# x1 stored to the output early, and the rectified sum added to it by accumulating transfers from GpSimd

## The reference

```python
def _gn(v, G=32, eps=1e-05): ...      # normalised over groups of 4 channels
x = x + _L0_conv_ref(_gn(x), ...)     # deformable 3x3 convolution, normalised over 8 channels
x = x + _L1_conv_ref(_gn(x), ...)     # below; its input is the normalised x

q1 = ternary_quantize(w1)
out1 = jax.nn.relu(batchnorm(conv3x3(x, q1), gamma1, beta1))
q2 = ternary_quantize(w2)
out2 = batchnorm(conv3x3(out1, q2), gamma2, beta2)
return jax.nn.relu(out1 + out2)
```

## Time and profile before

| | us |
|---|---|
| median of 3 runs | 325.41 (324.12 to 326.25) |
| the profiled execution's own time | 327.61 |
| its span, first to last instruction | 325.9 |
| PE busy | 277.9 (85%) |
| DVE busy | 209.8 (64%) |
| ACT busy | 177.1 (54%) |
| POOL busy | 145.1 (45%) |

### The profile page before, as it was taken

The page is one execution under the profiler, slowest core; times in us unless marked ns, Lnnn a source line. Parts: engine busy times, 40 slices in busy tenths (PEclk is TensorE's granted clock), DMA queues, the critical chain, the costliest instruction groups (busy, mean ns, idle before and its releaser), DMA issues.

```text
span 325.9 us, 4979 instructions
## 1 busy us (share of the span) xinstructions
PE 277.9 (85%) x1708; PEld 242.8 (75%) x1708; DVE 209.8 (64%) x416; ACT 177.1 (54%) x333; POOL 145.1 (45%) x195
## 2 busy tenths in 40 slices
PE   2889995859999989998998989999799976999900
PEld 1667774749998989998998989998577755777600
DVE  3788465557998799868878788883054625016196
ACT  2435832487876877977788777781033006221051
POOL 7340360647776668795656966421000004012053
PEclk9999999599999999999999999999799995999975
DMA  7801549823233232333323333200000000000015
GB/s 253 298 0 65 163 161 318 233 61 114 87 108 119 89 121 59 114 113 95 103 71 109 98 111 103 72 0 5 5 0 0 2 0 0 1 0 2 0 53 206
DMA packets 24887, 28.60 MB, mean 88 GB/s; under 512 B 2445, under 2 KB 22525, under 8 KB 24856
## 3 DMA queue, kind: packets, MB, share of 16 engines
q1 hardware_dynamic: 24640, 27.50, 26.4%
q10 hardware_dynamic: 216, 0.71, 0.8%
HBM read 19.87 MB, written 6.78 MB: 82 GB/s over the span
## 4 chain that ended last, share of the span: by engine, by line
PE 56%; DVE 17%; ACT 10%; SPq 8%; DMA 4%; issue 3%; DVEq 0%; ACTq 0%
PE PS L656 23%; PE PS L544 8%; PE PS L580 4%; PE PS L582 4%; PE PS L581 4%; PE PS L562 4%; PE PS L563 4%; PE PS L564 4%; SPq L349 3%; SPq L337 3%; DVE slo L1103 3%; DVE st L1007 2%; DVE vlo L1110 2%; ACT vhi L801 2%; ACT shi L794 2%
## 5 line engine op out<-in xcount | busy, mean ns | idle before, releaser
L443 POOL TENSOR_TENSOR vt<-rowm,hat 128x1026 f32<-128x1026 f32 x36 | 70.8, 1968 | 40.9 <-PE PS L544 40.5
L1103 DVE TENSOR_TENSOR slo<-PS,shi 114x512 fp32r<-114x512 f32 x72 | 53.9, 753 | 16.6 <-ACT shi L794 16.4
L794 ACT ACTIVATE shi<-PS 114x512 fp32r<-114x512 f32 x72 | 46.6, 652 | 23.9 <-PE PS L544 23.5
L1110 DVE TENSOR_TENSOR vlo<-PS,vhi 128x576 fp32r<-128x576 f32 (+2 forms) x84 | 50.0, 618 | 14.7 <-ACT vhi L801 14.6
L544 PE MATMUL PS<-ident,vt 128*114 128x128 f32 x324 | 49.5, 283 | 6.5 <-DVE xtt L1195 4.2
L801 ACT ACTIVATE vhi<-PS 128x576 fp32r<-128x576 f32 (+2 forms) x84 | 44.1, 546 | 7.8 <-PE PS L564 5.4
L562 PE MATMUL PS<-shi,patch 114*128 114x288 f32 x136 | 44.3, 325 | 3.4 <-DVE vlo L1110 3.3
L656 PE MATMUL PS<-xhi,q 128*128 128x512 f32 x144 | 41.3, 437 | 5.1 <-ACT xhi L941 5.1
L544 PEld LDWEIGHTS PS<-ident,vt 128*114 128x114 f32 x324 | 37.9, 140 | 9.8 <-issue 5.8
L580 PE MATMUL PS<-vhi,wdhi 128*128 128x256 f32 x144 | 43.0, 298 | 2.1 <-ACT xb L808 2.0
L563 PE MATMUL PS<-slo,patch 114*128 114x288 f32 x136 | 41.0, 302 | 0.0
(11 more groups left out here) (141 smaller groups left out, 472.8 us busy)
## 6 DMA issues: line engine op xcount, KB each, us to landing
patch<-xt SPq DMA_DIRECT2D x136, 114.0 KB
xt<-xtt SPq DMA_DIRECT2D x4, 1024.0 KB, 7.3
xs<-in_x SPq DMA_DIRECT2D x4, 512.0 KB, 7.8
out<-xb SPq DMA_DIRECT2D x8, 256.0 KB, 2.1
wraw<-in_L_conv_w SPq DMA_DIRECT2D x2, 576.0 KB, 10.6
omr<-omr SPq DMA_DIRECT2D x8, 128.0 KB, 5.0
wd_raw<-in_L_conv_weight ACTq DMA_DIRECT2D x1, 576.0 KB, 8.0
omr<-omr SPq DMA_DIRECT2D x4, 124.0 KB, 4.9
```

The costliest lines, as they stand in the source:

```text
L443: g.tensor_tensor(vt[:, n % 2, :, :].rearrange("p t (r j) -> p t r j", r=WR), rowm[:, n % 2, :, :].unsqueeze(3).to_broadcast([P, TAPS, WR, ...
L794: a.activation(shi[:, n % 2, lo:hi], S_PS[:, lo:hi], ACT.Copy).then_inc(shi_ok, 1)
L1103: d.tensor_tensor(slo[:, n % 2, lo:hi], S_PS[:, lo:hi], shi[:, n % 2, lo:hi], ALU.subtract).then_inc(slo_ok, 1)
L1110: last = d.tensor_tensor(places(vlo), src, places(vhi), ALU.subtract)
```

## The change

SyncE no longer stores the results. Behind the patches it stores x1 itself, one transfer of 128 x 1024 for each image, as soon as `x1_ok` says that the image is whole; each has a semaphore of its own, `x1_out`. In the tail every chunk goes one way: VectorE forms scale * conv + r1 into `xb`, ScalarE rectifies it with the shift as its bias, and GpSimd issues a transfer that adds the chunk to what the output holds, after a wait for that image's `x1_out`. SyncE waits for these eight (`out_done`) at the end, as before. GpSimd's adds of r1 + x1 during the second convolution are gone.

```diff
-            for n in OUT_ORDER:
-                sp.wait_ge(out_ok[n], 1)
-                sp.dma_start(out_v[:, n // 2, (n % 2) * BIG:(n % 2 + 1) * BIG], ychunk(n)).then_inc(out_done, 16)
+            for b in range(B):
+                sp.wait_ge(x1_ok, 2 * b + 2)
+                sp.dma_start(out_v[:, b, :], xs[:, b, :]).then_inc(x1_out[b], 16)
             sp.wait_ge(out_done, 16 * 2 * B)
...
-            for n in DVE_CHUNKS:
-                pool.wait_ge(r1_ok, n + 1)
-                g.tensor_tensor(ychunk(n), chunk(r1, n), chunk(xs, n), ALU.add).then_inc(rx_ok, 1)
-            for m, n in enumerate(POOL_CHUNKS):
-                pool.wait_ge(f_act, m + 1)
-                g.tensor_tensor(ychunk(n), ychunk(n), chunk(r1, n), ALU.add).then_inc(f_sum, 1)
-            pool.wait_ge(f_relu, B)
-            g.tensor_tensor(ychunk(n), ychunk(n), chunk(xs, n), ALU.add).then_inc(out_ok[n], 1)
+            for n in range(2 * B):
+                if n % 2 == 0:
+                    pool.wait_ge(x1_out[n // 2], 16)
+                pool.wait_ge(f_relu, n + 1)
+                pool.dma_start(out_v[:, n // 2, (n % 2) * BIG:(n % 2 + 1) * BIG], ychunk(n),
+                               accum_op=ALU.add).then_inc(out_done, 16)
...
-            for n in POOL_CHUNKS:
-                a.activation(ychunk(n), PS[:, n, :], ACT.Identity, bias=shift_of(BN2, 0),
-                             scale=scale_of(BN2, 0)).then_inc(f_act, 1)
-            for m, n in enumerate(POOL_CHUNKS):
-                act.wait_ge(f_sum, m + 1)
-                a.activation(ychunk(n), ychunk(n), ACT.Relu).then_inc(f_relu, 1)
+            for n in range(2 * B):
+                act.wait_ge(f_scaled, n + 1)
+                a.activation(ychunk(n), ychunk(n), ACT.Relu, bias=shift_of(BN2, 0)).then_inc(f_relu, 1)
...
-            scaled(0)
-            for m in range(B):
-                if m < B - 1:
-                    scaled(m + 1)
-                n = DVE_CHUNKS[m]
-                dve.wait_ge(f_scaled, m + 1)
-                d.scalar_tensor_tensor(out=ychunk(n), in0=ychunk(n), scalar=shift_of(BN2, 0),
-                                       in1=chunk(xs, n), op0=ALU.add, op1=ALU.max).then_inc(out_ok[n], 1)
-                if m:
-                    n = POOL_CHUNKS[m - 1]
-                    dve.wait_ge(f_relu, m)
-                    d.tensor_tensor(ychunk(n), ychunk(n), chunk(xs, n), ALU.add).then_inc(out_ok[n], 1)
+            for n in range(2 * B):
+                d.scalar_tensor_tensor(out=ychunk(n), in0=PS[:, n, :], scalar=scale_of(BN2, 0), in1=chunk(r1, n),
+                                       op0=ALU.mult, op1=ALU.add).then_inc(f_scaled, 1)
```

More of the change, by code:

```diff
@@ L188, in build @@
         r1_ok, r1hi_ok, r1lo_ok = sem("r1_ok"), sem("r1hi_ok"), sem("r1lo_ok")
[L189 to L194, removed]
+        f_scaled, f_relu, out_done = (sem(n) for n in ("f_scaled", "f_relu", "out_done"))
+        x1_out = [sem(f"x1_out{b}") for b in range(B)]
         v_bias, v_gamma, v_beta, v_g1, v_be1, v_g2, v_be2 = (vec[:, i:i + 1] for i in range(7))
@@ L1367, in _ @@
             dve.wait_ge(gn_ok, order(BN2, 0) + 1)
-            def scaled(m):
-                n = DVE_CHUNKS[m]
-                dve.wait_ge(rx_ok, m + 1)
-                d.scalar_tensor_tensor(out=ychunk(n), in0=PS[:, n, :], scalar=scale_of(BN2, 0),
-                                       in1=ychunk(n), op0=ALU.mult, op1=ALU.add).then_inc(f_scaled, 1)
-            scaled(0)
-            for m in range(B):
-                if m < B - 1:
-                    scaled(m + 1)
-                n = DVE_CHUNKS[m]
-                dve.wait_ge(f_scaled, m + 1)
-                d.scalar_tensor_tensor(out=ychunk(n), in0=ychunk(n), scalar=shift_of(BN2, 0),
-                                       in1=chunk(xs, n), op0=ALU.add, op1=ALU.max).then_inc(out_ok[n], 1)
-                if m:
-                    n = POOL_CHUNKS[m - 1]
-                    dve.wait_ge(f_relu, m)
-                    d.tensor_tensor(ychunk(n), ychunk(n), chunk(xs, n), ALU.add).then_inc(out_ok[n], 1)
+            for n in range(2 * B):
+                d.scalar_tensor_tensor(out=ychunk(n), in0=PS[:, n, :], scalar=scale_of(BN2, 0), in1=chunk(r1, n),
+                                       op0=ALU.mult, op1=ALU.add).then_inc(f_scaled, 1)
 _INS = ["x", "L0_conv_w_off", "L0_conv_b_off", "L0_conv_weight", "L0_conv_bias", "L0_conv_gamma", "L0_conv_beta",
```

## The result

The changed kernel takes 331.13 us (median of 4 runs, 330.0 to 333.46) against 325.83 us for the kernel before (324.12 to 327.09). The ratio is 1.0175, with a 95% interval of 1.0101 to 1.0249. Timed again on another occasion it was 1.0127 (1.0088 to 1.0165), 330.58 against 326.18 us. Both intervals lie above 1, so it is slower, by some 4 to 5 us.

A forecast was written before the change was run, and what follows sets the result against it. Bound by TensorE's second convolution to 309.2 us, then VectorE's tail; eight accumulating transfers at 1.4 us would land last at 327.2, 1.7 us later, so 325.41 + 1.7, rounded to 327.0 us; range 321.5 to 333.5.

The forecast's parts named there:

- the two rivals: Tail: GpSimd's issue becomes the bound (33%), 330.7 to 333.7 us; VectorE keeps GpSimd from issuing (5%), 331.4 us.
- Why VectorE was slow: Tail before the change: L1381 takes 1.09 or 1.75 us, the long ones lying beside or overlapping a GpSimd add.
- VectorE done after 5.7 us, at 0.705 a chunk, undisturbed: Tail: eight L1372-form instructions take 0.74 + 7 x 0.705 = 5.7 us, so VectorE ends at 317.8 instead of 322.65.
- GpSimd's adds in the second convolution cost nothing: Second convolution: L463's adds lengthen VectorE's L1362, but TensorE's work hides it with 2.3 us to spare.
- x1 stores free: Behind the patches: four stores, 5.7 us of transfer, land by about 252 us, awaited at 313.5; cost nothing.
- Start of the accumulations: Tail: first rectified chunk ready at 313.5 us, after 312.09 + 0.74 + 0.63 + about 0.04; GpSimd's issues begin there.
- Pace p, 1.4 us: Tail: slower of GpSimd's issue and the transfer, per chunk; transfer 2 x 0.71 = 1.42; last landing 314.6 + 9p = 327.2.
- the 15.5 of my sum: Predicted tail: the 13.8 us before the change, with the last landing 1.7 us later.
- The issue as the bound: GpSimd's queue in the tail: issues of 1.8 to 2.1 us set the pace, loss over 1% from p = 1.58; 33%.
- a sign of being wrong: End of the tail: the forecast is wrong if the final wait after the last issue exceeds 3 us.
- the case that I had put between -1% and +1%: Forecast's own case: accumulating transfers' pace p between 0.85 and 1.58 us, giving 322.1 to 328.7 us; 47%.
- VectorE keeps GpSimd from issuing: Tail: GpSimd issues nothing until VectorE is done at 317.8; landing at 331.5, 331.4 us for the median; 5%.

## Why the prediction came out as it did

The time lay in the range (321.5 to 333.5), but past the forecast of 327.0 and on the far side of the 1% that I had called likeliest to hold (47%, against 38% for slower). That it lay in the range owes something to luck: the range is 12 us wide, from a gain of 1% to a loss of 2.5%, and 331.13 is also what the two rivals gave that the runs refuted (330.7 to 333.7 for the issue, 331.4 for VectorE). Only the experiments tell them from the forecast's own mechanism. By steps:

- *Why VectorE was slow.* Only partly right. The one at 313.4 took 1.34 us, neither 1.09 nor 1.75, and short ones lie beside GpSimd's adds too. Here GpSimd adds from 312.95 to 319.23, and L1381 takes its shortest time in the midst:

```profile
312.95 6.28 POOL L466 TENSOR_TENSOR xb<-xb,r 128x512 f32<-128x512 f32 x4 [17.99 <-ACT xb L945]
...
315.35 1.09 DVE L1381 SCALAR_TENSOR_TENSOR xb<-xb,nsm,xs 128x512 f32<-128x512 f32 x1
```

- *VectorE done after 5.7 us, at 0.705 a chunk, undisturbed.* Nearly right: 5.36 us, 0.74 us each, 0.66 apart. The 0.705 was half of two instructions' 1.41 us; the distance between them is 1.41 - 0.74 = 0.67, which would have given 5.4 us. ScalarE's rectification takes 0.72 us in its new form, not 0.63, and still doesn't bind. The chain to the last landing was right as a whole: the kernel with plain stores from SyncE gives 8.9 us where the steps gave 8.8.
- *GpSimd's adds in the second convolution cost nothing.* Not shown. They lie ahead of the tail, so the tails can't tell, and their removal wasn't tried alone.
- *x1 stores free.* Right (1.0011, tail 13.8 us).
- *Start of the accumulations.* Too early. I let the first issue begin as the first rectification ended and its bytes 1.4 us later, 2.8 us after the first scaled chunk; they began at 314.5 - 310.83 = 3.7 us after it. GpSimd took up the issue 0.66 us after ScalarE's first chunk ended (311.68 + 0.72 = 312.40, to 313.06), and the first bytes came 1.4 us after that. The prediction had nothing for these 0.66 us; with 0.2 for the longer rectification they make 0.9 us of the miss.
- *Pace p, 1.4 us.* This is the mis-sized term: it measured 1.53 us. That the transfers bind, at about twice a store's time, was right; that the second read is the reason wasn't measured. The Trainium skill's factor of two ("Collectives: The Full Stack", the bandwidth ceiling) agrees with the end of the burst, from 322 us on: 200 GB/s against 381, a factor of 1.9. But up to 322 us it was 158, so the mean is 12.2 us for eight, 1.53 each, and 1.0 us of the miss. The prediction also had no term for the row length, which moves the engines' time from 13.3 to 11.6 us with 4 KB rows. With the first bytes' delay this is nearly all of the 2.0 us by which the tail of 17.5 exceeds the 15.5 of my sum. The timed difference, 4 to 5 us, is larger than the profiled one's 3.7 to 4.3, within its interval.
- *The issue as the bound.* I had set 1.4 us for it, from GpSimd's adds, and let the loss over 1% hang on it. It costs 0.91 us and doesn't bind. That both prices said 1.4 was chance; the sum stood because the slower of the two was the transfer. As the issues ran ahead of the bytes, the wait behind the last issue is over 6 us (320.3 to the last bytes at 326.7), more than the 3 us that the prediction had named as a sign of being wrong. The loss over 1% came instead from the case that I had put between -1% and +1%: its own mechanism, with both terms a little dearer. The edge of that case (p = 1.58) lay too near the forecast for 47%.
- *VectorE keeps GpSimd from issuing.* Wrong, as the 5% had it: 7.26 us with and without VectorE. What the Trainium skill says in "SBUF — State Buffer", on who interferes with whom, isn't contradicted, as no instruction of the kind that it warns of stands in this tail.

## What to carry to other kernels

Adding into an output by accumulating transfers trades vector work for DMA time: 0.6 us of VectorE a chunk here for 0.8 us more of the DMA engines, and the tail behind the last result is where those engines are needed. Count the engines' time for the last burst before counting what the vector engine saves. Where two engines slow each other on adds with both operands in the same memory, try the helper's adds beside instructions that read one operand from the matmul's banks; the version that did so had a tail 2.5 us shorter and a time 1.3 us shorter, without moving a byte more. And read the pace of merged instructions as (time of the group - one duration) / (count - 1), not as time over count.

## What the runs showed of the hardware

- An accumulating transfer of 128 rows costs GpSimd 0.87 to 1.02 us to issue whether the rows are 1, 2 or 4 KB; a plain one 0.54 us, and SyncE 0.33.
- Full DMA engines moved 352 to 381 GB/s of plain stores. With accumulations in 2 KB rows they moved 172 in the mean: 104 to 193 in the first 7 us or so, then about 200; with 1 KB rows 146.
- Accumulating the same 2.1 MB took the engines 11.6, 13.3 and 16.6 us in 576, 1,152 and 2,304 packets; plain stores took 5.7 us in 640 and 5.6 in 1,152.
- Behind a rectified chunk GpSimd's first issue began 0.66 us later, and the first bytes of an accumulation 1.4 us after that.
- GpSimd's plain stores were cut into 640 packets, its accumulating ones and SyncE's stores of the same bytes into 1,152.
- The old bytes that an accumulation must read are in no count of the profile: 19.87 MB read with and without the accumulations.
